# State scan of a two-layer sequence kernel: GpSimd makes the feed of the second channel half for every state

## The reference, cut to what matters

```python
A = -jnp.exp(A_log)
def step(h, inp):
    x_l, d_l, B_l, C_l = inp
    A_bar = jnp.exp(d_l[:, :, None] * A)
    h = A_bar * h + (d_l * x_l)[:, :, None] * B_l[:, None, :]
    y_l = jnp.einsum('ben,bn->be', h, C_l)
    return (h, y_l)
```

## Time and profile before

| | us |
|---|---|
| median of 3 runs | 3840.64 (3838.98 to 3842.27) |
| the profiled execution, its own time | 3842.64 |
| its span in the profile | 3840.9 |
| state scan of batch 0, first load issued to last VectorE instruction | 94.84 to 328.33 |
| state scan of batch 1, the same | 459.39 to 695.50 |
| busy: TensorE 3385.8, VectorE 2400.9, ScalarE 1681.7, GpSimd 2763.9 | |

### The profile page before, as it was taken

The page is one execution under the profiler, slowest core; times in us unless marked ns, Lnnn a source line. Parts: engine busy times, 40 slices in busy tenths (PEclk is TensorE's granted clock), DMA queues, the critical chain, the costliest instruction groups (busy, mean ns, idle before and its releaser), DMA issues. The chain is left out here.

```text
span 3840.9 us, 48142 instructions
## 1 busy us (share of the span) xinstructions
PE 3385.8 (88%) x18865; PEld 1747.3 (45%) x18865; DVE 2400.9 (63%) x2741; ACT 1681.7 (44%) x2037; POOL 2763.9 (72%) x1152
## 2 busy tenths in 40 slices
PE   5674677289999999999998599999999999995988
PEld 2222222245554555545454245555454554553766
DVE  5998699766666666666662665666666666642534
ACT  4331433144444554544544254545444455452433
POOL 1783188148888888888898198888888888893322
PEclk9997799689999999999999799999999999997989
DMA  1330233000000000000000100000000000001000
GB/s 25 133 113 22 65 114 104 27 3 1 4 1 4 4 1 4 1 4 2 1 1 10 33 1 4 1 4 1 4 4 1 4 1 1 1 1 55 12 18 9
DMA packets 61543, 76.24 MB, mean 20 GB/s; under 512 B 7289, under 2 KB 48962, under 8 KB 61250
## 3 DMA queue, kind: packets, MB, share of 16 engines
q1 hardware_dynamic: 57826, 72.03, 5.8%
q10 hardware_dynamic: 3488, 1.10, 0.1%
HBM read 66.30 MB, written 6.82 MB: 19 GB/s over the span
## 5 line engine op out<-in xcount | busy, mean ns | idle before, releaser
L1297 POOL TENSOR_TENSOR den_g<-den_g,p 128x1024 f32<-128x1024 f32 x896 | 2128.7, 2376 | 288.7 <-ACT p L1273 183.5
L964 DVE TENSOR_REDUCE quarters<-psum 128x2 f32<-128x1024 f32 x1024 | 1250.5, 1224 | 938.8 <-PE psum L957 935.7
L1273 ACT ACTIVATE p<-psum 128x1024 f32<-128x1024 f32 x1024 | 995.0, 1023 | 724.5 <-PE psum L1176 716.5
L1187 PE MATMUL psum<-p,v 128*64 128x512 f32 x4096 | 991.3, 605 | 0.0
L957 PE MATMUL psum<-k_main,q_main 64*128 64x512 f32 x2048 | 462.2, 446 | 13.7 <-DVE quarters L964 11.2
L1187 PEld LDWEIGHTS psum<-p,v 128*64 128x64 f32 x4096 | 248.5, 136 | 469.4 <-issue 315.6
L1176 PE MATMUL psum<-q_main,k_main 64*128 64x512 f32 x2048 | 407.5, 394 | 4.5 <-PEq L1087 4.5
L1176 PE MATMUL psum<-q_rest,k_main 64*128 64x512 f32 x2048 | 404.4, 390 | 0.0
L1176 PE MATMUL psum<-q_main,k_rest 64*128 64x512 f32 x2048 | 404.3, 390 | 0.0
L1176 PE MATMUL psum<-row_shift,row_ones 64*128 64x512 f32 x2048 | 403.8, 389 | 0.0
L957 PEld LDWEIGHTS psum<-k_main,q_main 64*128 64x128 f32 x2048 | 193.3, 184 | 362.5 <-issue 198.7
(11 more groups left out here) (242 smaller groups left out, 3291.0 us busy)
## 6 DMA issues: line engine op xcount, KB each, us to landing
c_sb<-bc_rows SPq DMA_DIRECT2D x64, 512.0 KB, 3.5
work<-bc_rows SPq DMA_DIRECT2D x32, 512.0 KB, 4.8
resid<-in_resid SPq DMA_DIRECT2D x8, 256.0 KB, 3.6
x_mid<-resid SPq DMA_DIRECT2D x8, 256.0 KB, 2.6
xa<-x_mid SPq DMA_DIRECT2D x8, 256.0 KB, 3.8
x_tok<-x_mid SPq DMA_DIRECT2D x8, 256.0 KB, 3.5
x_mid<-x_tok SPq DMA_DIRECT2D x8, 256.0 KB, 2.6
x<-x_mid SPq DMA_DIRECT2D x8, 256.0 KB, 2.8
```

The lines of the kernel that those rows point to most:

```text
L964: return nc.vector.reduce_max(quarters[:, :, n], max_banks.rearrange("p (h k) -> p h k", h=2), X_AXIS)
L1187: last = nc.tensor.matmul(o_bank[hi(h), :], vv[:, kt, hi(h)], p[:, u % LIVE, h, :], start=(kt == 0), stop=(kt == KT - 1))
L1273: nc.scalar.activation(flat(p[:, u % LIVE]), s_bank(u), ACT.Exp, scale=float(DH) ** -0.5).then_inc(p_ready, 1)
L1297: nc.gpsimd.tensor_tensor(sums, first, src, ALU.add).then_inc(added_g, 1)
```

## The change

`by_pool` answers yes for half 1 of every item, odd or even. So the 32 feeds of half 1 of a batch all come from GpSimd and none from VectorE; TensorE leaves out `replicate` for half 1 altogether; ScalarE writes every decay of half 1 to PSUM; SyncE loads a row of B for every item. GpSimd's queue becomes feed(0), feed(1), seen(0), feed(2), seen(1), feed(3), seen(2), and so on: the feed is made one item ahead in place of two, and its wait for a free slot of `fed` is written for that.

```diff
@@ -527,7 +527,7 @@
 def by_pool(i, h):
 
-    return h == 1 and i % 2 == 1
+    return h == 1
 
@@ -697,13 +697,13 @@
                     if k >= SLOTS:
 
-                        pool.wait_ge(scanned1, i - 2 * SLOTS + 1)
+                        pool.wait_ge(scanned1, i - SLOTS + 1)
                     nc.gpsimd.tensor_tensor(fed[:, k % SLOTS, :], dx[:, 1, s * SCAN:(s + 1) * SCAN], b_sb[:, k % SLOTS, :],
                                             ALU.mult).then_inc(fed_by_pool, 1)
 
-                feed(1)
+                feed(0)
                 for i, (s, n) in enumerate(items):
-                    feed(i + 2)
+                    feed(i + 1)
                     for h in range(EH):
                         pool.wait_ge(scanned[h], i + 1)
                     pool.wait_ge(c_loaded[i % C_SLOTS], 16 * (i // C_SLOTS + 1))
```

## The result

The changed kernel takes 3846.96 us, the median of 20 runs (3839.11 to 3855.41), against 3840.55 of the kernel before (3832.53 to 3844.89, 20 runs). The ratio is 1.0019, with a 95% interval of 1.0012 to 1.0025: 0.19% slower, just inside the 0.2% that was called no change, but clear of zero and outside the forecast range of 3829.5 to 3840.5. Its runs lie 16 us apart, from the fastest to the slowest; those of the kernel before lie 12 apart.

What follows compares the result with a forecast made beforehand. VectorE set the first piece's pace before; GpSimd would afterwards. Start, middle and end sum to -2.1 (batch 0) and -4.0 (batch 1), together -6 us from 3840.64: 3834.6. Its own range was 3831 to 3839; the stated range 3829.5 to 3840.5.

Steps and rivals of the forecast that it cites:

- the sentence on VectorE: First piece: VectorE needs 6.00 us against a pitch of 6.80; its spare 0.8 goes on waiting for GpSimd's port.
- the rival of the copy that loses its turn: Carry copy between feed and `seen`: if `seen` goes first, 3.6 us lost per miss, four making 0.2%; 5 in 100.
- The odd items show in advance what every item will be: GpSimd's queue: odd items, where `seen`, feed, `seen` run without waiting, 6.80 us together, are the pattern for every item.
- The floor: Middle, `seen`(0) to `seen`(30): GpSimd's pitch 6.80 us in the first piece, 6.79 in the second, 203.9 in all.
- SyncE's loads: Row of B: wanted 11.3 us after it is asked for, landing takes 4.9, so hidden; C has four items of lead.
- the five long stretches: Second piece, two scans: two-item stretches some 1.65 us long from sums at TensorE's lower clock go, each gaining 1.2.
- TensorE's clock: Rival: less work per item keeps TensorE at its lower clock level more than half the time; +10 us and up, 3 in 100.
- no replication that VectorE needs at once is behind it any more: TensorE's queue: reason why a lower-clock sum, 1.7 us more for its first half, ends in the slack.
- no wait of VectorE for L586: Sign to look for: in the second piece VectorE never waits for `replicate`, though single 3.6 us sums may remain.
- The end: `seen`(30) to VectorE's last instruction: `finish` gets the port first; 18.9 us, gaining 1.0 in batch 0, 1.7 in batch 1.
- The start: First load to `seen`(0): load taken as 3.8 us, `seen`(0) at 8.65 (8.35 to 9.75); losses of 1.0 and 0.7.

Runs made afterwards that it cites:

- the pause at every eighth item: Changed kernel, with GpSimd's `seen` waiting for the carry copy of its item at items 7 and 15 of the first piece: 3842.03 us, ratio 1.0000.
- the first piece alone: Half of the change against the kernel before: GpSimd makes every half 1 feed in the first piece, only odd ones in the second: 3860.40 us, ratio 1.0058.
- the second piece alone: Half of the change against the kernel before: GpSimd makes every half 1 feed in the second piece, only odd ones in the first: 3837.00 us, ratio 0.9992.
- a pause at every fourth item: Changed kernel, with `seen` waiting for the carry copy of its item at items 3, 7, 11, 15 of the first piece: 3836.14 us, ratio 0.9989.
- The kernel with the reduction: Changed kernel, with the carry taken by a one-column reduction in place of VectorE's copy: 3827.22 us, ratio 0.9967; run again 3829.74, 0.9972.

## Why the prediction was wrong

*The step that failed* is the sentence on VectorE, that it spends its 0.8 us "waiting for the port, as it does in the odd items now", and with it the rival of the copy that loses its turn, put at 5 in 100 because "it won its turn in all 16 odd items". In the sum such a loss stood at nothing; the four of the profile cost 21.5 us and turned a gain of 8 in the scans into a loss of 13.5. The rival had the right mechanism with the right price for one loss (3.6 forecast, 3.6 measured in 3 of the 8) and too small a one for the others, which lost a second time, to the feed behind `seen` (5.9 to 6.3). The chance was wrong. To have asked first is no claim to the turn: the copy had been waiting since 141.96 when `seen` started at 142.84. The 16 wins had all come under one condition that the change removes: GpSimd had waited for VectorE shortly before, at most three instructions back. "The odd items show in advance what every item will be" holds for the durations and not for the turn.

What the runs show of that condition: in the profiles of the changed kernel, of the pause at every eighth item and of the first piece alone there are 13 lost turns. Before each the copies since GpSimd's last wait had won 3 to 12 times in a row (5, 7, 6, 3, 5, 4, 3, 4 in the changed kernel's two profiles). Of the 54 meetings among the first three after a wait none was lost, of the 51 from the fourth on 13 were. In 48 meetings with a wait in each pair (the kernel before twice, and the second piece alone) and 22 with a pause at every fourth item, none was lost. That it takes an unbroken run of GpSimd is thus well supported.

The run is not the whole of it, and the place has a part: 5 of the 13 losses are at item 12. From the fourth meeting after a wait on, its copy lost 5 of 7, all others together 8 of 44. The copy before it stands out too. In item 11 of the changed kernel's first piece a scan of VectorE starts 0.49 us late, and the copy waits 0.6 us in place of 0.95; so it is in seven of the eight scans of these four profiles, all but the one where item 10 had just lost:

```profile
175.28 2.29 DVE L661 TENSOR_TENSOR_SCAN state<-a_bar,psum 128x1024 f32<-128x1024 f32 x1 [0.49 <-ACT a_bar L624]
...
179.85 0.59 DVE L686 COPY carry<-state 128x2 f32<-128x2 f32 x1
```

The place alone does not do it either: with a pause at every fourth item, item 12 is the first after a pause, and it won both times. Why a run is needed, why a loss comes at the fourth meeting once and at the thirteenth another time, and what item 12 has to do with it stays open. Between the copy that lost at 141.96 and the one that won at 135.17 no row shows a difference.

*The floor was right.* Steps of `seen` of 6.79 in both pieces, where 6.80 and 6.79 were forecast. VectorE kept up, SyncE's loads were in time, and the five long stretches of the second piece went. Without the late items the profile has 8.9 + 203.6 + 18.4 = 230.9 us for the scan of batch 0, where 8.65 + 203.9 + 18.9 = 231.4 had been worked out, and 230.8 for batch 1. The scans would be 7.9 shorter; 6 were forecast.

*TensorE's clock* does fall in the changed kernel, and in batch 0 three such falls show on VectorE, in batch 1 six (1.05 to 1.26 us each). One of them, in the timelines of the two engines:

```profile
258.88 6.66 PE L598 MATMUL psum<-seen,ident 128*128 128x512 f32 x8 [2.43 <-POOL seen L712]
```

```profile
266.24 1.23 DVE L643 TENSOR_TENSOR psum<-dx,psum 128x1024 f32<-128x1024 f32 x1 [2.63 <-PE psum L586]
```

Nearly the whole sum ran at half speed, 6.66 us in place of 3.70, and VectorE waited 2.63 us for the replication behind it. GpSimd did not notice: its steps there are 6.78. That rival was rightly priced as hidden, but not for the reason given, that "no replication that VectorE needs at once is behind it any more": one for half 0 is, and what hides the wait is that VectorE was ahead of GpSimd. So the test "no wait of VectorE for L586" was too strict.

*The end.* `finish` did not get the port first, as was assumed: it was asked for in the middle of `seen`(30) and lost the turn behind it to `seen`(31) (8.80 for its two instructions, and 8.95 for two `seen`, undisturbed). So it did in all 18 scans of the nine profiles in which GpSimd makes every feed of the second piece. At this boundary, from `seen` straight to `seen`, the waiting VectorE instruction lost every time. It cost nothing, since the last `seen` was over earlier: 18.4 us from `seen`(30) in place of 18.9.

*The start.* The row of B was there 3.95 us after its issue (97.17 - 93.22), 3.8 had been taken. The range of the prediction was also added up wrongly: a start of up to 1.1 us more in each batch is +2.2 and not +2.6, and its terms give 3830 to 3841, not 3831 to 3839. The measured time is outside either.

*What stays open in size.* The kernel with the reduction is 11 to 12 us faster than the kernel before by the medians, more than the shorter scans account for: 462.5 and 461.7 us for the two scans in its two profiles, against 469.6 and 467.9 before, 5 to 8 less. The rest of the span is 3365.1 and 3367.0 us in these two, 3371.3 and 3367.9 in those of the kernel before; it differs by 2 to 3 us between two profiles of one kernel, and no experiment looked at the difference that remains.

## What to carry to other kernels

When a change makes GpSimd busy without a break, look for every VectorE instruction that waits for GpSimd's end now, however small it is: a copy of two columns lasted 7.7 us and held the pipeline up for 6. A stall that always resolved the same way is evidence only for the conditions under which it was seen; ask which of them the change takes away. If a small move between two such engines can be written as an instruction that takes 0.155 us beside a busy GpSimd, write it so before making GpSimd the bound.

## What was not expected of the hardware

A VectorE instruction and GpSimd's do not take turns. With a copy waiting in the changed kernel, GpSimd's next instruction won 8 of 53 times at the end of a feed, and then again 5 of 8 times at the end of `seen`; in the kernel before it never did in 32. From one `seen` straight to the next it won 18 of 18 times, against `finish`. A reduction of the same two columns (0.155 us) never waited, nor did ScalarE's copy of them (0.176 us). And time taken from VectorE in the kernel before (0.6 us a pair) came back in full as half-speed sums of TensorE.
